# The inversion's last level by products, pair additions and identity sums in PSUM, with the value and gate projections ahead of it

## What is computed

```python
x = x + 0.5 * ffn(layernorm(x)); x = x + attn(layernorm(x)); x = x + 0.5 * ffn(layernorm(x))
```

```python
bS = einsum('bhk,bhkv->bhv', b_t, S)
S = exp(g)[..., None] * S + a_t[..., None] * bS[:, :, None, :] + k_t[..., None] * v_t[:, :, None, :]
o = einsum('bhk,bhkv->bhv', q_t, S)
```

## Time and profile before

| | us |
|---|---|
| median of 3 runs (lowest, highest) | 1971.96 (1968.42, 1979.21) |
| the profiled execution, its own time | 1968.42 |
| its span, from first to last instruction | 1966.6 |
| TensorE busy | 1525.7 (78%) |
| VectorE busy | 1165.4 (59%) |
| ScalarE busy | 780.1 (40%) |
| GpSimd busy | 755.4 (38%) |
| mean granted TensorE clock | 0.863 |

### The profile page before, as it was taken

One profiled execution on the slowest core, in us unless ns is written; L12 is line 12 of the kernel. 1 busy time (PEld: TensorE's weight loads), 2 busy tenths in 40 slices (PEclk: granted clock), 3 DMA queues, 4 the chain that ended last, 5 costly groups with the idle time before them and its releaser, 6 DMA issues. The chain is left out here.

```text
span 1966.6 us, 68546 instructions
## 1 busy us (share of the span) xinstructions
PE 1525.7 (78%) x26124; PEld 1291.1 (66%) x26125; DVE 1165.4 (59%) x3492; ACT 780.1 (40%) x1805; POOL 755.4 (38%) x912
## 2 busy tenths in 40 slices
PE   5499999998656478555886647776577799999995
PEld 5499999997235365343753525545365799999994
DVE  7546444443287777767777696767956346444442
ACT  1243333332466235562345643356433243333331
POOL 2555322222075251572413725228344123522221
PEclk9999999999778598786687967878757899999998
DMA  9553322222101000010000001000100653333224
GB/s 302 182 158 86 73 48 48 48 48 38 54 7 47 22 21 22 6 46 25 22 22 4 24 27 38 17 10 12 41 12 11 217 161 60 84 68 49 47 48 109
DMA packets 84242, 116.31 MB, mean 59 GB/s; under 512 B 12952, under 2 KB 74464, under 8 KB 82016
## 3 DMA queue, kind: packets, MB, share of 16 engines
q1 hardware_dynamic: 56224, 76.27, 12.2%
q0 software_dynamic: 27360, 37.80, 10.7%
q10 hardware_dynamic: 544, 0.86, 0.1%
HBM read 64.87 MB, written 54.21 MB: 61 GB/s over the span
## 5 line engine op out<-in xcount | busy, mean ns | idle before, releaser
L1059 POOL DMA_INDIRECT x<-ffn_yout,ffn_place x142 | 222.2, 1565 | 532.3 <-DVE ffn_yout L991 449.0
L997 DVE TENSOR_TENSOR ffn_inner<-ffn_inner,ffn_bank 128x512 f32<-128x512 f32 x142 | 97.5, 687 | 354.7 <-PE ffn_bank L871 352.3
L871 PE MATMUL ffn_bank<-ffn_tileT,ffn_gate_now 128*128 128x128 f32 x2272 | 280.2, 277 | 0.0
L871 PE MATMUL ffn_bank<-ffn_tileT,ffn_up_now 128*128 128x128 f32 x2272 | 278.3, 276 | 0.0
L881 PE MATMUL ffn_bank<-ffn_w,ffn_inner 128*128 x1136 | 268.9, 380 | 1.7 <-DVE ffn_yout L991 1.7
L871 PEld LDWEIGHTS ffn_bank<-ffn_tileT,ffn_gate_now 128*128 128x128 f32 x2272 | 268.4, 194 | 0.1
L952 ACT ACTIVATE ffn_inner<-ffn_bank 128x512 f32<-128x512 f32 x142 | 84.8, 597 | 459.9 <-PE ffn_bank L871 459.8
L871 PEld LDWEIGHTS ffn_bank<-ffn_tileT,ffn_up_now 128*128 128x128 f32 x2272 | 266.7, 193 | 0.0
L881 PEld LDWEIGHTS ffn_bank<-ffn_w,ffn_inner 128*128 128x128 f32 x1136 | 205.0, 190 | 24.4 <-issue 2.5
L814 ACT COPY ffn_gate_now<-ffn_w 128x1024 f32 x142 | 148.4, 1045 | 29.1 <-issue 21.9
L814 DVE COPY ffn_up_now<-ffn_w 128x1024 f32 x142 | 98.9, 696 | 52.6 <-issue 42.4
(11 more groups left out here) (493 smaller groups left out, 3114.0 us busy)
## 6 DMA issues: line engine op xcount, KB each, us to landing
ffn_w<-in_w1t_dram SPq DMA_DIRECT2D x16, 1024.0 KB, 5.4
ffn_tile<-xs SPq DMA_DIRECT2D x122, 130.0 KB, 2.1
ffn_w<-in_w2t_dram SPq DMA_DIRECT2D x16, 512.0 KB, 6.5
ffn_x<-in_x_dram SPq DMA_DIRECT2D x16, 256.0 KB, 5.8
x<-ffn_x SPq DMA_DIRECT2D x16, 256.0 KB, 5.7
pass_xa<-x SPq DMA_DIRECT2D x12, 256.0 KB, 3.2
pass_xr<-x SPq DMA_DIRECT2D x12, 256.0 KB, 2.6
x<-pass_xr SPq DMA_DIRECT2D x12, 256.0 KB, 2.2
```

What stands on the lines that cost most here:

```text
L871: t = pe.matmul(bank[:, i * P:(i + 1) * P], half_now[half][b][:, k, i * P:(i + 1) * P], rowsT[b][:, k * P:(k + 1) * P], start=(k == 0), st ...
L997: dve.tensor_tensor(inner[b][:, :], inner[b][:, :], p_u[b][:, :], ALU.mult).then_inc(s_act, 1)
L1059: pool.indirect_dma_start(total, bass.IndirectOffsetOnAxis(ap=place[b][:, 0:1], axis=0), yout[b][:, :], None, compute_op=ALU.add).then_inc ...
```

## The change

VectorE still forms every product of the last level, but adds only pairs: terms 3+4, 5+6, 7+8, 9+10, 11+12 and 13+14. The ten terms that are left (`TERMS`: 0, 1, 2, 3, 5, 7, 9, 11, 15, 13, where an odd one from 3 to 13 stands for its pair) are summed by TensorE, as matmuls with the identity that accumulate in PSUM: Z in `wide`, X in `psum[0]` (rows 0 to 7) and `psum[1]` (rows 8 to 15). `FORMED` says after how many VectorE instructions of a half each is there. A half is now 22 instructions. The products lie in a ring of seven buffers (three `pr`, `zz`, three in `a_top`); from term 7 on VectorE waits until TensorE has summed what lay there, on the new semaphore `s_acc`. X's products read Z from PSUM, and begin when all ten sums of Z are done. `compact` takes the lower half from PSUM.

TensorE's order is now: banks 0 to 3, the eight projections, then the sums with banks 4 to 9 between them, and banks 10 and 11 at the end. Banks 8 to 11 use `psum[4]` to `psum[7]`. ScalarE's order is banks 0 to 3, the table load and the projections, the first compaction, banks 4 to 7, and the rest as before. The level waits for all 18 groups (`s_ev`) before it begins, since the ring lies in `a_top`. The smaller levels are as they were.

```diff
+    TERMS = (0, 1, 2, 3, 5, 7, 9, 11, 15, 13)
+    FORMED = (1, 2, 3, 7, 10, 13, 16, 19, 21, 22)
+    PRODUCT, PARTS = FORMED[-1], len(TERMS)
+    ring = [pr[:, i, :] for i in range(3)] + [zz[:, :]] + [
+        a_top[:, :, :].rearrange("p g x -> p (g x)")[:, i * HQ * CT * CT:(i + 1) * HQ * CT * CT] for i in range(3)]
+    z_sum = env["wide"][:, :].rearrange("p (b j i) -> p b j i", b=HQ, j=CT)
+    x_sum = [psum[i][:, :].rearrange("p (b j i) -> p b j i", b=HQ, j=CT // 2) for i in range(2)]
+    def back_bank(n):
+        return psum[n] if n < 8 else psum[4 + n % 4]
...
-        for size, m in enumerate(SIZES):
+        for size, m in enumerate(SIZES[:-1]):
...
+        def zterm(x):
+            kk = CT - 1 - x
+            return eng.tensor_tensor(term(x)[:, :, :, 0:kk + 1], blk(ng, CT, CT, kk, kk + 1, di=0), blk(tm, kk, CT, 0, kk + 1, dj=0), ALU.mult)
+        def xterm(x):
+            rows = CT - x
+            return eng.tensor_tensor(term(x)[:, :, 0:rows, :], blk(tm, CT + x, rows, CT + x, CT, di=0), z_sum[:, :, x:x + 1, :].to_broadcast([P, HQ, rows, CT]), ALU.mult)
+        def zpair(x):
+            a, b = term(x)[:, :, :, 0:CT - 1 - x], term(x + 1)[:, :, :, 0:CT - 1 - x]
+            return eng.tensor_tensor(a, a, b, ALU.add)
...
+        eng.wait_ge(s_ev, GROUPS)
+        for p, one, two in ((0, zterm, zpair), (1, xterm, xpair)):
+            if p > 0:
+                eng.wait_ge(s_acc, PARTS)
+            for x in range(CT):
+                if 7 <= x <= 10:
+                    eng.wait_ge(s_acc, PARTS * p + x - 6)
+                elif x in (12, 14):
+                    eng.wait_ge(s_acc, PARTS * p + x // 2 - 1)
+                step(one(x))
+                if x in (5, 7, 9, 11, 13):
+                    step(two(x - 2))
+            step(two(CT - 3))
...
+            def total(p, y):
+                x = TERMS[y]
+                pe.wait_ge(s_inv, SMALL + PRODUCT * p + FORMED[y])
+                if p == 0:
+                    for half in range(2):
+                        heads = slice(half * HQ // 2, (half + 1) * HQ // 2)
+                        t = pe.matmul(z_sum[:, heads, :, 0:CT - x], ident[:, :], term(x)[:, heads, :, 0:CT - x],
+                                      start=(y == 0), stop=(y == PARTS - 1), skip_group_check=True)
+                else:
+                    H = CT // 2
+                    if x < H:
+                        pe.matmul(x_sum[0][:, :, x:H, :], ident[:, :], term(x)[:, :, 0:H - x, :],
+                                  start=(y == 0), stop=(x == H - 1), skip_group_check=True)
+                    first = max(x, H)
+                    t = pe.matmul(x_sum[1][:, :, first - H:H, :], ident[:, :], term(x)[:, :, first - x:CT - x, :],
+                                  start=(y == 0), stop=(y == PARTS - 1), skip_group_check=True)
+                t.then_inc(s_acc, 1)
+            pe.wait_ge(s_ev, GROUPS)
+            pe.wait_ge(s_aq, 3)
+            for n in range(4):
+                back(n)
+            for j, (t, g, c) in enumerate(VALUES):
...
+            pe.wait_ge(s_vale, len(VALUES))
+            for p in range(2):
+                for y in range(PARTS):
+                    total(p, y)
+                    if (p, y) == (0, 3):
+                        pe.wait_ge(s_tc, 2)
+                        back(4)
+                    elif (p, y) == (0, 5):
+                        back(5)
+                    elif (p, y) == (1, 2):
+                        back(6)
+                    elif (p, y) == (1, 4):
+                        back(7)
+                    elif (p, y) == (1, 6):
+                        pe.wait_ge(s_tc, 3)
+                        back(8)
+                    elif (p, y) == (1, 7):
+                        back(9)
+            pe.wait_ge(s_tc, 4)
+            back(10)
+            back(11)
...
+            act.wait_ge(s_inv, SMALL)
+            compact(slice(0, CT), slice(0, SUB))
+            compact(slice(CT, SUB), slice(CT, SUB))
+            for n in range(4, 8):
+                back(n)
+            act.wait_ge(s_acc, PARTS + TERMS.index(CT // 2 - 1) + 1)
+            compact(slice(CT, CT + CT // 2), slice(0, CT), x_sum[0])
+            for n in range(8, 10):
+                back(n)
+            act.wait_ge(s_acc, 2 * PARTS)
+            compact(slice(CT + CT // 2, SUB), slice(0, CT), x_sum[1])
```

More of the change, by code:

```diff
@@ L2002, in _, with back @@
                 t.then_inc(s_tp, 1)
[L2004 to L2024 removed]
+            def back(n):
@@ new lines, in _ @@
+            pe.wait_ge(s_ev, GROUPS)
[3 more added lines that the diff above has]
+            for j, (t, g, c) in enumerate(VALUES):
+                if j < 4:
+                    pe.wait_ge(s_bke, j + 1)
+                    for kc in range(KCH):
+                        t = pe.matmul(psum[j][:, :], wv[:, kc, g * P:(g + 1) * P], xT[:, kc, c * 512:(c + 1) * 512],
+                                      start=(kc == 0), stop=(kc == KCH - 1))
+                else:
+                    pe.wait_ge(s_vale, j - 3)
+                    t = pe.matmul(psum[j % 4][:, :], wrank[RANK:2 * RANK, g * P:(g + 1) * P], fg[RANK:2 * RANK, c * 512:(c + 1) * 512], start=True, stop=True)
+                t.then_inc(s_val, 1)
@@ L2065, in _, with compact, back @@
                 i.then_inc(s_ev, 1)
[L2067 to L2087 removed]
+            def compact(rows, cols, src=None):
+                src = tmv[:, :, rows, cols] if src is None else src
+                act.copy(tc[:, rows, :, cols], src.rearrange("p h j i -> p j h i")).then_inc(s_tc, 1)
+            def back(n):
                 act.wait_ge(s_bk, n + 1)
```

73 lines of the change are left out of this document (25 added, 48 removed).

## The result

| kernel and occasion | median (runs) | kernel before beside it | ratio [95%] |
|---|---|---|---|
| changed, first measurement | 2016.43 us (4) | 1974.03 us (4) | 1.0214 [1.0180, 1.0248] |
| changed, occasion 2 | 1978.54 (10) | 1963.98 (13) | 1.0052 [1.0021, 1.0084] |
| changed, occasion 3 | 2017.03 (4) | 1979.10 (7) | 1.0208 [1.0170, 1.0246] |
| changed, occasion 4 | 2019.24 (4) | 1973.18 (14) | 1.0245 [1.0203, 1.0288] |

The changed kernel is slower: by 2.1% in the measurement that the prediction is held against, where the forecast was 1973 us with a range to 1989. The same program, unedited, was measured on three more occasions (an occasion is a set of kernels timed together on one chip, with the kernel before among them). Twice the 2% came back; once it was 0.5%.

The account below looks back on a forecast made before the run. VectorE was taken to bound the last level, 42.4 us; after the change 24.3 + 18.8 = 43.1 us, +2.5 us for four passes, less 0.4 a pass in the scan: net +1 us, 1973 us, range 1961 to 1989.

Parts of the forecast that it names:

- What is moved: Last level, first half: sums queue behind projections running 0.1 to 12.6 us in; VectorE's second half starts at 24.3 us.
- The clock: TensorE in the level: clock rises during the projections and stays up while sums run; spread -0.9 to +2 us over passes.
- The second half: Last level from VectorE's second-half start to the last copy: 18.8 us against 22.8 before, with TensorE trailing.
- VectorE's 13.4 us: VectorE's own work in a half: 178 units in 22 instructions, 13.4 us, where a half took near 19.5.
- the 0.86 us for 512 columns: TensorE's sums: 0.86 us per 512 columns at 2.4 GHz, 10.1 us for a half's 6,016 columns.
- the stall at term 7: First half: VectorE reaches term 7 at 7.5 us and waits for term 0's sum until 14.7, a 7 us stall.
- TensorE as the bound of the first half: After the first half's stall TensorE sets the pace: 12.65 + 10.4 + 0.9 = 24.0 us.
- Rival A: Slower: TensorE falls to 1.2 GHz in the second half, 2018 us, or 1985 to 1997 in part; chance 0.20.
- Rival C: Faster: VectorE never waits in the first half, level 33.4 us, -9.0 a pass, 1934 us; chance 0.02.
- 15.3 us a half: VectorE's half if the skill's 151 cycles counted in full between starts; 2 us worse than 13.4, rejected from the trace.

Follow-up runs that it names:

- the version with the projections alone: Kernel before with only the projections moved ahead of bank 4: 1955.46 us (one run); timed again, 1974.22 us, ratio 1.0002.
- the repeat: The changed kernel measured again without an edit, on occasion 2: 1978.54 us, ratio 1.0052.
- the gates first: Changed kernel with the four gate projections ahead of the four value projections, sums waiting for the four Silus alone: 2018.58 us.
- the version with the projections last: Changed kernel with its eight projections behind bank 11 instead of ahead of the sums: 1968.17 us (one run).
- X-only version: Changed kernel with Z formed as before, projections back behind bank 7, only X by pairs and TensorE sums: 1939.09 us, ratio 0.988; again 1980.30 us, 1.0047.

## Why the prediction was wrong

A loss of half a per cent lay within the stated range, though the forecast itself was 0.05%; the other one and a half did not. By steps, for the third pass, in us of the level:

| step | predicted | occasion 2 | first measurement |
|---|---|---|---|
| level's start behind the small levels | none | 0.1 | 5.3 |
| projections start | 0.1 | -0.1 | 3.4 |
| first sum | 12.65 | 12.5 | 15.0 |
| VectorE's second half starts | 24.3 | 26.0 | 29.8 |
| second half to the last copy | 18.8 | 17.4 | 17.4 |
| level | 43.1 | 43.4 | 47.2 |

- **The step that failed** is under "What is moved": "TensorE is done with its first four banks as the level starts, so they run from 0.1 to 12.6 us into it". It took from the trace of before a margin, 18 groups copied 3.6 us ahead of the level, as if it were fixed; and that trace was of an execution without late signals. The change makes two new things hang on that margin: VectorE's wait for all groups, which the prediction never priced, and, through the banks and the projections, all sums. In the first measurement the groups are done 8.7 us later (5.8 to 10.9 over the twelve passes of the unedited changed kernel with late signals), and both cost: 5.3 us of standing and 2.4 us to the first sum. With VectorE adding everything and not waiting for the groups, 7.3 to 8.8 us of it are free, as the version with the projections alone shows. No rival held this; my bound of nothing for the groups' wait was a missing bound.
- **The clock at the start of the sums.** "The clock ... stay up while sums run" was wrong for their first 3 to 6 us. From the first sum to VectorE's second half it took 13.5 us instead of 11.65 in the repeat, which is all that this half was over, and 14.8 in the first measurement. With the gates first it took 11.85. The fall comes at the end of the gate projections, whose row at full clock I had read without asking what comes after it.
- **The second half** was 1.4 us shorter than my sum. I let TensorE stand 1 us for ScalarE's copy ahead of bank 8, because I had the copy wait for seven sums. It waits for six (term 7 is the sixth of `TERMS`); in the trace ScalarE copies while TensorE is in the seventh sum, and bank 8 starts 12.85 us in without a stand.
- **Right:** VectorE's 13.4 us for the second half (the first, broken by the stall, has 14.0); the 0.86 us for 512 columns; the stall at term 7 with TensorE's sum as its releaser; TensorE as the bound of the first half. Without late signals the stage grew by 1.0 to 1.6 us a pass against my 0.6, and the kernel by 0.5% [0.2, 0.8] against my 0.05%: half a per cent is ten times the forecast, and the level came as near as 0.3 us only because the slow start of the sums and the shorter second half offset each other.
- **Rival A** had the sign and not the mechanism: the clock is 1.00 in the second half of every trace of the changed kernel, and that its 2018 us lie near the measured 2016.43 is chance. The Trainium skill, TensorE: Matmul & The Clock Gate, section HAM oscillation, tells of groups of matmuls parted by waits that are throttled anew. Its example has longer waits than this second half, whose longest idle stretch of TensorE is 1.4 us, at its start; the clock stayed up here, which speaks neither for the page nor against it. **Rival C**, VectorE never waiting, happened in the version with the projections last (Z in 14.8 us where C had 14.6), and the projections then cost at the end what they had cost in the middle: C left out that they must go somewhere.
- VectorE: DVE Perf Modes of the Trainium skill, section on the TRN2 errata, with its 151 cycles beyond the elements, would have given 15.3 us a half if counted in full between starts; 22 instructions in 13.40 us show it is not.

## What to carry to other kernels

An operation may cost nothing where it stands because another engine is busy longer beside it. Count one that is moved off such a place twice: what it costs where it goes, and what covers the work that queues behind it. Here half the change (X alone) gains 1.2%, because Z's work on VectorE hides TensorE's projections, and doing Z the same way takes that cover away and turns the gain into a loss. And where an edit makes a path wait for work that merely used to be early, price its lateness, not only its mean: signals that put the groups off by 7 to 9 us were free in the version with the projections alone, and like ones cost the changed kernel 8 to 9 us a stage.

## What the runs showed of the hardware

- Signals from TensorE to ScalarE that follow each other in 0.45 us on some occasions come up to 2.9 us apart on others, over the first 21 us or so of the stage, with the same program, while TensorE's own records stay as they were. The gaps are near multiples of 0.72 us. The kernel before is some 0.5% slower on those occasions.
- The same lateness stands in the first feed-forward part beside GpSimd's scatters (a copy at 55.1 to 57.3 us instead of 45.6 to 46.8). In the attention stage it was gone once the scatters were put behind the transposes, and the X-only version then gained 1.2% on an occasion of the late kind, where it had lost 0.5% on another with the scatters in place.
- 16 increments of a semaphore ahead of TensorE's transposes delayed the first copy by 2.7 us and nearly doubled the distance of the next five; the stage grew by 3 to 5 us, for instructions that the profile does not count as busy.
- The granted clock fell to 1.2 GHz at the end of four matmuls of 32 rows although TensorE was busy without a break (4.00 of 4.00 us in the version with the gates first); in the changed kernel's second half, where TensorE is idle for 1.4 us at the start, it stayed at 2.4 GHz.
